# Later token placement in the expert phase and a one-bank, deeper pipeline in the second layer

## The chip, the cores and the metric

One Trainium2 chip, one of its cores. The metric is the device time of one execution in microseconds (us), the median over runs of the same kernel.

## What is computed

Sixteen sequences of 256 tokens with 256 features each (4096 tokens) pass two layers. The first is cross attention with 16 heads to a context of 120 rows per sequence, then a mixture of eight experts of which every token takes two. The second is cross attention with one head and a mask, then a linear layer whose input and weight are rounded in blocks of 32. All four parts are added to their own input, and each begins with a layer norm. Cut to its core:

```python
def reference(x, ctx_1024, mask_BxSxS2_ik1, ...):
    x = x + _L0_xattn_ref(_layernorm(x), ctx_1024, L0_xattn_Wq, L0_xattn_Wkv)
    x = x + _L0_ffn_ref(_layernorm(x), L0_ffn_W1, ..., L0_ffn_beta)
    x = x + _L1_xattn_ref(_layernorm(x), ctx_1024, ctx_1024, mask_BxSxS2_ik1, ...)
    x = x + _L1_ffn_ref(_layernorm(x), L1_ffn_weight, L1_ffn_bias)

def _L0_ffn_ref(...):
    probs = softmax(flat @ gate_W); topk_w, topk_idx = top_k(probs, 2)
    out = 0.5 * gelu(flat @ shared_W + shared_b)
    for e in range(8):
        out = out + combine[:, e:e+1] * (gelu(flat @ W1[e] + b1[e]) @ W2[e] + b2[e])
    # then a layer norm with gamma and beta

def _L1_xattn_ref(q, k, v, mask, Wq, Wk, Wv):
    Z = where(mask == 0, -1e9, (q@Wq) @ (k@Wk).T / 16);  return softmax(Z) @ (v@Wv)

def _L1_ffn_ref(x, weight, bias):
    xd, wd = rounded in blocks of 32 to a 6-bit grid, scaled back
    return xd @ wd.T + bias
```

## The kernel before

The program has three phases, one after the other on every engine: `attention_phase` (first layer's attention, up to about 305 us), `expert_phase` (to about 830 us) and `second_phase` (the rest). The order of the work on each engine is written out by hand. Engines meet only through semaphores: a wait blocks everything behind it on that engine.

**Expert phase.** The 8192 token copies are sorted by expert and cut into `SLOT_TILES` = 71 tiles of 128 rows. One tile n takes, on TensorE (PE), `first_product(n + 1)` (two halves of 16 matmuls), `turn_rows(n + 2)` (transposes of gathered rows) and `second_product(n)` (16 matmuls). VectorE (DVE) copies the tile's first weights (`tile_weights`, L1669) and adds bias and weight to the result (`finish`, L1682 and L1686). ScalarE (ACT) runs gelu (L1751).

Which rows a tile holds is found in two steps. `put` (L415, its DMA at L423) places 128 copies at a time: each of 128 descriptors writes 8 bytes (row number and weight) into the table `buckets` in DRAM. The first half of the tokens is placed during the attention phase, the second half (groups `THIRD` and `LAST`, 32 puts) in the expert loop on GpSimd (POOL). `slots` (L1426, on the SyncE queue SP) then fetches a tile's 128 entries into `b_slots`, in parts given by `PARTS`; with them POOL gathers the tile's rows (`gather`, L1509) and adds its results to `ffn_rows` in DRAM (`scatter`, L1520). Tiles 0 to 23 (`EARLY_TILES`) hold tokens of the first half alone; tile 24 and later need all puts to have landed.

POOL's loop over n: gather(n + 3), up to two puts, a scatter (from n = 9 on, two at every fourth n from 16), more puts. Puts start at n = `PUT_AT` = 5, with 5/2 a tile. The first puts wait for the places and weights that DVE makes at n = 4. In the same stretch SP carries 16 chunks of the shared branch through SBUF (load L1453, gelu on ACT L1460, store L1465), two chunks a tile up to n = 7; the first scatter waits until all are stored.

**Second phase.** It works on 16 batches of 256 tokens, each engine in `CYCLES` of one batch at several stages. For a batch n:

- DVE: `stats_acc`, `centre`, `residual` (L2058: x3, the input of the layer), `stats_x3`; `bounded` (L2089 scores with mask, L2093 maximum), `attended` (L2122: x4 = x3 + attention / sum of probabilities), `stats_x4`, `scales` (block maxima L2102 to L2109)
- POOL: `inverse_std` three times (norms of acc, x3, x4), `to_blocks` (L2004), `scale_back` (L2013)
- ACT: `normalise_x3` and `normalise_x4` (both L2154), `exps` (L2199), copies out of PSUM: `keep_xnT` (L2175), `keep_probsT` (L2209), `keep_xdT` (L2225), `keep_result` (L2232); `round_blocks` (L2217) and `lay_bias` (L2241, which writes the bias into the result's PSUM bank)
- PE: `turn_rows` (L2315), `scores` (L2345), `turn_probs` (L2355, transposes), `weigh` (L2365, attention times values), `start_result` (L2285, adds x4 to the result's bank by an identity matmul), `turn_quantised` (L2275), `linear` (L2295)

Of each context come keys (L2324) and values (L2332), after a transpose (L2303). The first `EARLY` = 7 contexts are worked before the cycles, while the last scatters land; contexts 7 to 15 inside them, one a cycle.

Of the kernel before, what the change touches and what calls it, by code (L numbers as in the profile page):

```python
# [1327 lines left out]
def expert_phase(nc, sem, past, routing, starts, ident, w1_sb, w2_sb, b1_rows, s_b12, b2, s_w1, s_w2,  # L1328
# [9 lines left out]
    with st:  # L1338
# [3 lines left out]
        def ps(name, shape, dt=F32):  # L1342
# [9 lines left out]
                 (EARLY_TILES, 40), (40, NS))  # L1352
# [50 lines left out]
        PUT_AT = 5  # L1403
# [109 lines left out]
        def gpsimd(pool):  # L1513
# [17 lines left out]
            for n in range(1, NS):  # L1531
                if n + AHEAD - 1 < NS:
# [3 lines left out]
                        range(5 * at // 2, min(5 * (at + 1) // 2, 4 * routing.GT))  # L1536
# [256 lines left out]
def second_phase(nc, sem, past, ident, second, mask, x2_d, acc_d, ctx, out):  # L1793
# [7 lines left out]
    with st:  # L1801
# [26 lines left out]
        x4, xn4 = ring("c_x4_", T2, n=2), ring("c_xn4_", T2, n=2)  # L1828
# [5 lines left out]
        tie = sb("c_tie", [P, 1])  # L1834

# [29 lines left out]
        g_bank = ps("c_g_ps", [P, 512])  # L1865
        g_ps = g_bank[:, 0:KC * CTX].rearrange("p (k c) -> p k c", k=KC)
# [3 lines left out]
        o_ps = ps("c_o_ps", T2)  # L1870
        xdT_ps = ps("c_xdT_ps", [P, 2, KC, P])
        f_ps = ps("c_f_ps", T2)
# [24 lines left out]
        s_o_p = sem("c_attn_psum")  # L1897
        s_rs = sem("c_rs_ready")
        s_x4 = sem("c_x4_ready")
        s_xn4 = sem("c_xn4_ready")  # L1900
        s_fb = sem("c_result_bias_set")
# [24 lines left out]
        CYCLES = range(-3, B + 3)  # L1926
# [3 lines left out]
        EARLY = 7  # L1930
# [4 lines left out]
        def sync(sp):  # L1935
# [25 lines left out]
            for n in range(RING):  # L1961
                load_x2(n)
            for s, value in past["added"]:
                sp.wait_ge(s, value)
            for n in range(RING):
                load_acc(n)
            for n in range(CTX_RING, B):
                load_context(n)
            for c in CYCLES:
# [3 lines left out]
                if exists(c + 5) and c + 5 >= RING:  # L1973
                    load_acc(c + 5)
                    load_x2(c + 5)
            for i in range(2):
                sp.wait_ge(s_ost[i], 8 * B)

        def gpsimd(pool):
# [38 lines left out]
            pool.memset(tie[:], TIE * FP8_DOWN).then_inc(s_tie, 1)  # L2018
            for c in CYCLES:
                scale_back(c - 2)  # L2020
                inverse_std(N4, c - 1, s_xn4)
                inverse_std(N3, c + 1, s_xn3)
                to_blocks(c - 1)
                inverse_std(NA, c + 3, s_x3)

        def vector(dve):
# [23 lines left out]
            def residual(n):  # L2050
# [5 lines left out]
                dve.wait_ge(s_x2_in[n % RING], loaded(n))  # L2056
                for u in range(2):
# [18 lines left out]
            def stats_x4(n):  # L2076
                if not exists(n):
                    return
                dve.wait_ge(s_x4, n + 1)
                stats(N4, x4[n % 2], n)  # L2080
# [30 lines left out]
            def attended(n):  # L2111
                if not exists(n):
                    return
                i = n % 2
                dve.wait_ge(s_e, n + 1)
                dve.reciprocal(rs[i][:], psum_[i][:]).then_inc(s_rs, 1)
                dve.wait_ge(s_rs, n + 1)
                dve.wait_ge(s_o_p, n + 1)
                ge(dve, s_f_p, n - 1)
                ge(dve, s_xn4, n - 1)  # L2120
                for u in range(2):
                    j = dve.scalar_tensor_tensor(out=x4[i][:, u, :], in0=o_ps[:, u, :],  # L2122
                                                 scalar=rs[i][:, u:u + 1], in1=x3[n % RING][:, u, :],
                                                 op0=ALU.mult, op1=ALU.add)
                j.then_inc(s_x4, 1)
# [13 lines left out]
            for c in CYCLES:  # L2139
                bounded(c)  # L2140
                stats_acc(c + 3)
                residual(c + 2)
                scales(c - 1)
                stats_x3(c + 2)
                attended(c)
                stats_x4(c)
                centre(c + 3)

        def scalar(act):
# [14 lines left out]
            def normalise_x4(n):  # L2164
# [3 lines left out]
                normalise(N4, xn4, x4, n, s_xn4)  # L2168
# [14 lines left out]
            def keep_keys(n):  # L2183
                act.wait_ge(s_g_p, n + 1)
                act.copy(gT[n][:], g_ps).then_inc(s_g, 1)
# [17 lines left out]

            def keep_probsT(n):
# [6 lines left out]
            def round_blocks(n):  # L2211
                if not exists(n):
                    return
                act.wait_ge(s_tie, 1)
# [12 lines left out]
            def keep_result(n):  # L2227
# [4 lines left out]
                act.copy(o[n % 2][:], f_ps[:]).then_inc(s_o, 1)  # L2232

            def lay_bias(n):
                if not exists(n):
                    return
                if n == 0:
                    act.wait_ge(second["s_vec"], 32)
                    act.wait_ge(s_fb, 1)
                ge(act, s_o, n)  # L2240
                act.copy(f_ps[:], fb[:].unsqueeze(1).broadcast_to(T2)).then_inc(s_fb, 1)  # L2241
# [7 lines left out]
            for c in CYCLES:  # L2249
                n = c + EARLY  # L2250
                exps(c)
                normalise_x4(c - 1)
                if late(n + 2):
                    keep_keys(n + 2)
                keep_probsT(c)
                normalise_x3(c + 1)
                keep_result(c - 2)
                lay_bias(c - 1)
                if late(n + 3) and n + 3 > EARLY:
                    keep_context(n + 3)  # L2260
                round_blocks(c - 1)
                keep_xnT(c + 1)
                if late(n + 1):
                    keep_values(n + 1)
                keep_xdT(c - 1)

        def tensor(pe):
            def turn_quantised(n):
                if not exists(n):
                    return  # L2270
                pe.wait_ge(s_xd, n + 1)
# [7 lines left out]
            def start_result(n):  # L2279
                if not exists(n):  # L2280
                    return

                pe.wait_ge(s_x4, n + 1)
                pe.wait_ge(s_fb, n + 2)
                pe.matmul(f_ps[:].rearrange("p u d -> p (u d)"), ident[:],  # L2285
                          x4[n % 2][:].rearrange("p u d -> p (u d)"),
# [133 lines left out]
```

## Time and profile before

| | us |
|---|---|
| median of 3 runs | 990.2 (989.22 to 990.7) |
| the profiled execution | 992.3 |
| its span, first to last instruction | 990.5 |
| PE busy | 934.2 (94%) |
| DVE busy | 530.0 (54%) |
| ACT busy | 517.7 (52%) |
| POOL busy | 495.2 (50%) |

The page's 40 slices show busy tenths per slice of 24.8 us:

```profile
PE   6999999999989979999999999999999999898885
DVE  3787898788874533452322323222232323899972
ACT  4777777677754723333343333333333333588774
PEclk9999999999999989999999999999999999999999
```

PE is full through the expert phase (slices 13 to 33), but for slice 15 (347 to 371 us), where it shows a 7 and the granted clock an 8. In the last six slices, the second phase, DVE is as full as PE or fuller.

### The profile page before, as it was taken

The numbers are of one execution on the slowest core, as the hardware profiler recorded it, in microseconds if no ns is written. First come the engines' busy times: TensorE is split into PE (matmuls) and PEld (weight loads), VectorE is DVE, ScalarE is ACT, GpSimd is POOL, SyncE is SP. The second block draws the span as 40 slices with busy tenths as digits, with TensorE's granted clock in tenths as the row PEclk, the third lists the DMA queues.
The fourth block names the chain that finished last, engine by engine and source line by source line (L and its number), as shares of the span: only waits on it lengthen the run. The fifth ranks groups of instructions, "written<-read, shape, count | busy, mean of one in ns | idle before, by whom it ended". The sixth has DMA issues, their size and how long they took to land. (4 is left out here: it accounts for less than half of the span.)

```text
span 990.5 us, 22054 instructions
## 1 busy us (share of the span) xinstructions
PE 934.2 (94%) x7133; PEld 797.3 (80%) x7133; DVE 530.0 (54%) x1300; ACT 517.7 (52%) x1310; POOL 495.2 (50%) x659
## 2 busy tenths in 40 slices
PE   6999999999989979999999999999999999898885
PEld 4777777676768969989999999999999998676653
DVE  3787898788874533452322323222232323899972
ACT  4777777677754723333343333333333333588774
POOL 3444344565653155775554443434444442577773
PEclk9999999999999989999999999999999999999999
DMA  5244453354533354433432221222222227433301
GB/s 179 77 124 149 134 177 122 114 152 141 151 118 108 115 136 68 53 32 47 55 59 44 38 44 27 32 40 32 44 33 39 38 41 188 129 97 97 96 33 43
DMA packets 86127, 85.39 MB, mean 86 GB/s; under 512 B 19296, under 2 KB 81184, under 8 KB 85888
## 3 DMA queue, kind: packets, MB, share of 16 engines
q1 hardware_dynamic: 70336, 65.28, 22.1%
q0 software_dynamic: 15680, 18.69, 12.8%
q8 instruction: 62, 1.02, 0.5%
q14 instruction: 49, 0.40, 0.2%
HBM read 52.54 MB, written 31.39 MB: 85 GB/s over the span
## 5 line engine op out<-in xcount | busy, mean ns | idle before, releaser
L1751 ACT ACTIVATE b_hiddenT<-b_H,b_b 128x128 f32<-128x128 f32 x568 | 161.8, 368 | 330.2 <-PE b_H L1581 293.8
L1581 PEld LDWEIGHTS b_H<-b_rowsT,b_w 128*128 128x128 f32 x2272 | 265.5, 192 | 12.2 <-issue 5.3
L1581 PE MATMUL b_H<-b_rowsT,b_w 128*128 128x128 f32 x2272 | 267.5, 275 | 6.4 <-issue 4.1
L1602 PE MATMUL b_Y<-w_sb,b_hiddenT 128*128 x1136 | 258.4, 381 | 1.1 <-ACT b_hiddenT L1751 0.6
L1520 POOL DMA_INDIRECT ffn_rows<-b_y,b_slots x71 | 140.5, 1979 | 197.2 <-DVE b_y L1686 121.1
L1602 PEld LDWEIGHTS b_Y<-w_sb,b_hiddenT 128*128 128x128 f32 x1136 | 211.5, 191 | 27.6 <-issue 1.4
L1682 DVE TENSOR_TENSOR b_y<-b_Y,b_b 128x256 f32<-128x256 f32 x71 | 30.2, 425 | 309.6 <-PE b_Y L1602 260.7
L1669 DVE COPY b_w<-w_sb 128x2048 f32 x71 | 87.3, 1230 | 35.5 <-issue 31.7
L1509 POOL DMA_INDIRECT b_rows<-xn_rows,b_slots x71 | 75.7, 1067 | 53.7 <-PE b_xT L1570 33.7
L1243 ACT COPY a_probsT<-a_T 120x512 f32<-120x512 f32 x128 | 74.7, 585 | 47.7 <-PE a_T L939 38.5
L423 POOL DMA_INDIRECT buckets<-r_pay,r_place x64 | 68.3, 1067 | 47.0 <-DVE r_pay L373 20.4
L939 PE MATMUL a_T<-ident,a_probs 128*120 128x128 f32 x512 | 77.9, 280 | 3.3 <-ACT a_probs L1235 3.1
L1076 DVE TENSOR_REDUCE a_max<-a_S 128x8 f32<-128x960 f32 x64 | 73.6, 1150 | 13.1 <-PE a_S L919 12.7
L1084 DVE TENSOR_TENSOR a_probs<-a_S,a_max 128x960 f32<-128x960 f32 x64 | 73.2, 1144 | 0.7
L939 PEld LDWEIGHTS a_T<-ident,a_probs 128*120 128x120 f32 x512 | 57.5, 139 | 16.0 <-issue 9.3
L1235 ACT ACTIVATE a_probs<-a_probs 128x960 f32<-128x960 f32 x64 | 64.5, 1007 | 8.3 <-DVE a_probs L1084 6.4
L953 PE MATMUL a_O<-a_probsT,a_vaug 120*32 120x128 f32 x1024 | 54.7, 287 | 0.5 <-ACT a_probsT L1243 0.3
L953 PEld LDWEIGHTS a_O<-a_probsT,a_vaug 120*32 120x32 f32 x1024 | 20.4, 108 | 29.3 <-issue 23.5
L785 POOL TENSOR_TENSOR a_x<-a_x,a_xin 128x256 f32<-128x256 f32 x16 | 12.4, 772 | 49.0 <-DVE a_x L1097 44.0
L988 PE MATMUL a_M<-a_wsg,a_xn2T 128*128 128x264 f32 x128 | 35.6, 401 | 0.2 <-ACT a_xn2T L1258 0.2
L919 PE MATMUL a_S<-a_kbd,a_qT 32*128 32x240 f32 x512 | 35.0, 387 | 0.9 <-ACT a_qT L1219 0.8
L2154 ACT ACTIVATE c_xn<-c_x,c_x_nb,c_x_rstd 128x256 f32<-128x256 f32 x64 | 34.8, 593 | 0.4 <-POOL c_x_nb L1995 0.3
(232 smaller groups left out, 1293.6 us busy)
## 6 DMA issues: line engine op xcount, KB each, us to landing
w_sb<-in_L_ffn_W SPq DMA_DIRECT2D x32, 512.0 KB
x_rows<-a_x SPq DMA_DIRECT2D x32, 128.0 KB
xn_rows<-a_xn SPq DMA_DIRECT2D x32, 128.0 KB
shared_rows<-a_shared SPq DMA_DIRECT2D x32, 128.0 KB
b_spare<-shared_rows SPq DMA_DIRECT2D x16, 256.0 KB
ffn_rows<-b_spare SPq DMA_DIRECT2D x16, 256.0 KB
c_x<-x_rows SPq DMA_DIRECT2D x16, 256.0 KB
c_acc<-ffn_rows SPq DMA_DIRECT2D x16, 256.0 KB, 2.9
```

Source lines behind the costliest of these rows:

```text
L423: pool.indirect_dma_start(bucket_d, IndirectOffsetOnAxis(place[:, t, k:k + 1], 0), pay[:, t, k, :], None).then_inc(s_put[g // 2], 16)
L939: i = pe.transpose(T_ps[q % 2][0:CTX, j * P:(j + 1) * P], pr[q // 2][:, 4 * (q % 2) + j, :], ident[:])
L953: i = pe.matmul(O_ps[VB * j:VB * (j + 1), q * P:(q + 1) * P], vaug[t // 2 % 2][0:CTX, 4 * q + j, :], pT[q % 2][0:CTX, j, :], start=True, s ...
L1076: dve.tensor_reduce(mx[h][:].rearrange("p (r j) -> p r j", r=RG), scores_of(h), AX.X, ALU.max).then_inc(s_mx, 1)
L1084: dve.tensor_tensor(pr[h][:].rearrange("p (r j) c -> p r j c", r=RG), scores_of(h), mx[h][:].rearrange("p (r j) -> p r j", r=RG).unsqueeze ...
L1243: act.copy(pT[q % 2][0:CTX].rearrange("p j n -> p (j n)"), T_ps[q % 2][0:CTX, :]).then_inc(s_T, 1)
L1509: pool.indirect_dma_start(xg[n % AHEAD][:], None, xn2_d, IndirectOffsetOnAxis(iw[:].bitcast(I32)[:, n, 0:1], 0)).then_inc(s_x[n % AHEAD], 16)
L1520: pool.indirect_dma_start(acc_d, IndirectOffsetOnAxis(iw[:].bitcast(I32)[:, n, 0:1], 0), y[n % KEPT_Y][:], None, bounds_check=TOK + SPARE - 1,
L1581: j = pe.matmul(H_ps[i][:, c * P:(c + 1) * P], w1c[i][:, k * HID + c * P:k * HID + (c + 1) * P], xT[:, k * P:(k + 1) * P], start=(k == 0), ...
L1602: j = pe.matmul(y_ps[i][:, 0:D], hT[i][:, c * P:(c + 1) * P], w2_sb[:, bass.ds(e * (HB * D) + c * D, D)], start=(c == 0), stop=(c == HB - 1))
L1669: dve.tensor_copy(w1c[i][:], w1_sb[:, bass.ds(e * (KC * HID), KC * HID)])
L1751: j = act.activation(hT[i][:, c * P:(c + 1) * P], H_ps[i][:, c * P:(c + 1) * P], ACT.Gelu, bias=b1c[i][:, c:c + 1])
```

## The change

1. **Placement.** `PUT_AT` goes from 5 to 8 and the rate from 5/2 to 8/3 puts a tile, so the puts are issued at n = 8 to 19 (before: 5 to 17). `PARTS` cuts the last 47 tiles into (24, 28), (28, 44), (44, 71) where it had (24, 40), (40, 71).
2. **One PSUM bank a batch.** There are three result banks `f_ps`. `start_result` (now first) lays x3 into the batch's bank, `weigh` adds attention to it there (making x4 in PSUM), and `linear` adds a bias matmul (one row of ones times the bias, 512 columns) and the four products. DVE's `attended` and its SBUF tile x4 are gone, and ACT's `lay_bias` too. `stats_x4` and `normalise_x4` read the bank.
3. **Division by the sums.** `inverse_sums` (DVE) takes the reciprocal, `diagonals` (ACT, two activations 128x128) makes a diagonal matrix of it, and `turn_probs` becomes a matmul with that matrix in place of the identity.
4. **Order.** The pipeline is one or more cycles deeper (`range(-4, B + 4)`), and every engine's order is new. `EARLY` is 9; a late context's keys and values are copied by ACT a cycle after PE made them; late keys share a bank with the contexts' transposes. SP loads contexts 8 and 9 ahead of the wait for the last scatter, and accumulator rows three cycles earlier.

```diff
-        PARTS = (..., (19, EARLY_TILES), (EARLY_TILES, 40), (40, NS))
+        PARTS = (..., (19, EARLY_TILES), (EARLY_TILES, 28), (28, 44), (44, NS))
-        PUT_AT = 5
+        PUT_AT = 8
-                        range(5 * at // 2, min(5 * (at + 1) // 2, 4 * routing.GT))
+                        range(8 * at // 3, min(8 * (at + 1) // 3, 4 * routing.GT))
...
-        EARLY = 7
+        EARLY = 9
...
             for c in CYCLES:      # POOL
-                scale_back(c - 2)
-                inverse_std(N4, c - 1, s_xn4)
-                inverse_std(N3, c + 1, s_xn3)
-                to_blocks(c - 1)
-                inverse_std(NA, c + 3, s_x3)
+                inverse_std(NA, c + 3, s_x3)
+                inverse_std(N3, c + 2, s_xn3)
+                to_blocks(c - 1)
+                inverse_std(N4, c, s_xn4)
+                scale_back(c - 1)
...
             for c in CYCLES:      # DVE
                 bounded(c)
-                stats_acc(c + 3)
                 residual(c + 2)
+                inverse_sums(c)
+                stats_x3(c + 2)
+                centre(c + 3)
                 scales(c - 1)
-                stats_x3(c + 2)
-                attended(c)
+                stats_acc(c + 4)
                 stats_x4(c)
-                centre(c + 3)
...
+            def diagonals(n):     # ACT
+                act.wait_ge(s_rs, n + 1)
+                for u in range(2):
+                    j = act.activation(dg[n % 2][:, u, :], ident[:], ACT.Identity,
+                                       scale=rs[n % 2][:, u:u + 1])
+                j.then_inc(s_dg, 1)
...
             for c in CYCLES:      # ACT, all lines new
+                exps(c - 1)
+                normalise_x4(c - 2)
+                diagonals(c - 1)
+                if late(c + 9):
+                    keep_keys(c + 9)
+                keep_result(c - 4)
+                keep_probsT(c - 1)
+                if late(c + 9):
+                    keep_values(c + 9)
+                keep_xdT(c - 3)
+                keep_xnT(c)
+                if EARLY < c + 10 < B:
+                    keep_context(c + 10)
                 normalise_x3(c + 1)
+                round_blocks(c - 2)
...
             def start_result(n):  # PE
-                pe.wait_ge(s_x4, n + 1)
-                pe.wait_ge(s_fb, n + 2)
+                pe.wait_ge(s_x3, n + 1)
+                ge(pe, s_o, n - 2)
                 # identity times x3 (before: x4), start=True
             def linear(n):
                 pe.wait_ge(s_xdT, n + 1)
+                pe.matmul(f_ps[n % RING][:], ones[0:1, :],
+                          fb[0:1, :].unsqueeze(1).broadcast_to([1, 2, D]),
+                          start=False, stop=False, skip_group_check=True)
...
             for c in CYCLES:      # PE, all lines new
+                turn_quantised(c - 3)
+                turn_probs(c - 1)
+                start_result(c - 1)
+                weigh(c - 1)
+                if EARLY < c + 10 < B:
+                    turn_context(c + 10)
+                scores(c)
+                linear(c - 3)
                 turn_rows(c + 1)
+                if late(c + 10):
+                    keys(c + 10)
+                if late(c + 10):
+                    values(c + 10)
```

## Rows read from the trace of the kernel before

**Rows 1.** Windows: stretch, its length, then busy us (instructions) of PE, PEld, DVE, ACT, POOL, granted PE clock, DMA share, GB/s. Expert phase.

```profile
600.00:700.00 100.00, 100.00 (x695) 94.40 (x694) 29.20 (x56) 34.56 (x123) 43.09 (x26) 1.00 0.22 35
...
331.55:339.15 7.60, 7.60 (x61) 7.17 (x60) 4.19 (x14) 4.84 (x12) 0.00 (x0) 1.00 0.25 71
...
346.40:355.29 8.89, 7.92 (x62) 7.06 (x61) 4.07 (x13) 2.60 (x10) 6.98 (x7) 1.00 0.63 141
355.29:371.82 16.53, 10.74 (x50) 8.96 (x51) 3.82 (x14) 4.47 (x13) 7.43 (x8) 0.79 0.54 137
371.82:379.07 7.25, 7.25 (x52) 6.83 (x50) 2.08 (x4) 2.54 (x9) 4.62 (x4) 1.00 0.43 96
```

**Rows 2.** Timeline, 338 to 376 us: start, length, engine, line, instruction, idle before.

```profile
343.11 1.05 POOL L423 DMA_INDIRECT buckets<-r_pay,r_place  x1 [20.40 <-DVE r_pay L373]
...
353.83 1.14 ACT L1751 ACTIVATE b_hiddenT<-b_H,b_b 128x128 f32<-128x128 f32 x4 [4.23 <-remote]
...
364.67 0.42 DVE L1682 TENSOR_TENSOR b_y<-b_Y,b_b 128x256 f32<-128x256 f32 x1 [12.66 <-remote]
...
373.54 2.61 POOL L1520 DMA_INDIRECT ffn_rows<-b_y,b_slots  x1 [8.68 <-issue]
```

**Rows 3.** DMA queues from 354 to 355 us: packets, MB, share of 16 engines.

```profile
q0 software_dynamic: 16, 0.07, 124.3%
```

**Rows 4.** Timelines of SP and POOL: the last 47 fetches of slots, the gather of tile 24.

```profile
446.58 53.16 SPq L1426 DMA_DIRECT2D b_slots<-buckets  x47
...
466.13 1.57 POOL L1509 DMA_INDIRECT b_rows<-xn_rows,b_slots  x1 [1.38 <-DMA b_slots<-buckets]
```

**Rows 5.** Windows of the second phase: four periods with contexts, eight without.

```profile
867.00:899.10 32.10, 30.59 (x185) 25.03 (x184) 29.90 (x101) 26.20 (x69) 23.14 (x49) 1.00 0.32 100
...
906.44:968.21 61.77, 49.80 (x262) 36.71 (x261) 52.92 (x184) 47.89 (x113) 44.12 (x94) 1.00 0.22 72
```

**Rows 6.** Groups by line, 845 to 990 us: busy us, mean ns of one, idle before.

```profile
L2122 DVE SCALAR_TENSOR_TENSOR c_x<-c_o_ps,c_rs,c_x 128x256 f32<-128x256 f32 x32 | 14.0, 480 | 2.6 <-PE c_o_ps L2365 2.0
...
L2058 DVE SCALAR_TENSOR_TENSOR c_x<-c_centred,c_acc_rstd,c_x 128x256 f32<-128x256 f32 x30 | 12.8, 467 | 0.0
L2199 ACT ACTIVATE c_probs<-c_z,c_nmax 128x120 f32<-128x120 f32 x32 | 12.4, 388 | 4.1 <-DVE c_nmax L2093 4.1
```

**Rows 7.** Timeline, a period without contexts: linear, weigh, and what PE starts next.

```profile
931.69 1.89 PE L2295 MATMUL c_f_ps<-c_wdT,c_xdT 128*128 128x256 f32 x8
...
933.42 1.03 PE L2365 MATMUL c_o_ps<-c_v,c_probsT 120*128 120x256 f32 x4
...
934.28 0.60 PE L2315 MATMUL c_xnT_ps<-ident,c_xn 128*128 128x128 f32 x4
```

**Rows 8.** Timeline, the second phase's beginning: rows, scores, z of batch 0, keys, values.

```profile
849.81 0.66 PE L2315 MATMUL c_xnT_ps<-ident,c_xn 128*128 128x128 f32 x4 [0.57 <-ACT c_xn L2154]
...
851.24 1.12 PE L2345 MATMUL c_zp_ps<-c_gT,c_xnT 128*128 128x120 f32 x8 [0.56 <-ACT c_xnT L2175]
...
852.20 1.06 PE L2324 MATMUL c_g_ps<-c_ctxT,c_wkq 128*128 128x120 f32 x8
852.40 0.41 DVE L2089 SCALAR_TENSOR_TENSOR c_z<-c_zp_ps,c_bound 128x240 f32<-128x240 f32 x1 [2.27 <-PE c_zp_ps L2345]
...
853.09 1.03 PE L2332 MATMUL c_v_ps<-c_wv,c_ctxT 128*120 128x256 f32 x4
```

**Rows 9.** Timeline, batch 15 to the end: z, stats and norm of x4, linear, result.

```profile
968.21 0.41 DVE L2089 SCALAR_TENSOR_TENSOR c_z<-c_zp_ps,c_bound 128x240 f32<-128x240 f32 x1 [0.81 <-PE c_zp_ps L2345]
...
974.07 0.75 DVE L2032 BATCH_NORM_STATS2 c_x_bn<-c_x 128x6 f32<-128x256 f32 x2
...
976.96 1.09 ACT L2154 ACTIVATE c_xn<-c_x,c_x_nb,c_x_rstd 128x256 f32<-128x256 f32 x2 [0.30 <-POOL c_x_nb L1995]
...
983.77 3.49 PE L2295 MATMUL c_f_ps<-c_wdT,c_xdT 128*128 128x256 f32 x8 [0.68 <-ACT c_xdT L2225]
987.30 0.59 ACT L2232 COPY c_out<-c_f_ps 128x512 f32<-128x512 f32 x1 [3.58 <-PE c_f_ps L2295]
```

More of the change, by code:

```diff
@@ L1869, in second_phase @@
         pT_ps = zp_ps[0:CTX, 256:512].rearrange("p (u n) -> p u n", u=2)
-        o_ps = ps("c_o_ps", T2)
-        xdT_ps = ps("c_xdT_ps", [P, 2, KC, P])
-        f_ps = ps("c_f_ps", T2)
+        f_ps = [ps(f"c_f_ps{i}", T2) for i in range(RING)]
         s_acc_in = [sem(f"c_acc{i}_loaded") for i in range(RING)]
@@ L1924, in loaded @@
             return 16 * (n // RING) + 16
-        CYCLES = range(-3, B + 3)
-        EARLY = 7
+        CYCLES = range(-4, B + 4)
+        EARLY = 9
         def late(n):
@@ L1962, in sync @@
                 load_x2(n)
+            for n in range(CTX_RING, CTX_RING + 2):
+                load_context(n)
             for s, value in past["added"]:
@@ L1966, in sync @@
                 load_acc(n)
-            for n in range(CTX_RING, B):
+            for n in range(CTX_RING + 2, B):
                 load_context(n)
-            for c in CYCLES:
+            for c in range(-5, B + 4):
                 if exists(c - 2):
@@ L2109, in scales, with inverse_sums @@
                 dve.reciprocal(rsc[i][:], sc[i][:]).then_inc(s_rsc, 1)
-            def attended(n):
+            def inverse_sums(n):
                 if not exists(n):
                     return
-                i = n % 2
                 dve.wait_ge(s_e, n + 1)
[L2116 to L2125, printed above, removed]
+                ge(dve, s_dg, n - 1)
+                dve.reciprocal(rs[n % 2][:], psum_[n % 2][:]).then_inc(s_rs, 1)
             def bounds(part):
@@ L2184, in keep_keys @@
                 act.wait_ge(s_g_p, n + 1)
-                act.copy(gT[n][:], g_ps).then_inc(s_g, 1)
+                act.copy(gT[n][:], late_g_ps if late(n) else early_g_ps).then_inc(s_g, 1)
             def keep_values(n):
@@ L2231, in keep_result @@
                 ge(act, s_ost[n % 2], 16 * (n // 2))
[L2232 to L2241, printed above, removed]
+                act.copy(o[n % 2][:], f_ps[n % RING][:]).then_inc(s_o, 1)
             load_exp_and_log(nc, act)
@@ L2320, in keys @@
                 pe.wait_ge(s_ctxT, n + 1)
-                ge(pe, s_g, n)
+                if not late(n):
+                    ge(pe, s_g, n)
+                at = late_g_ps if late(n) else early_g_ps
                 for m in range(KC):
                     for k in range(KC):
-                        j = pe.matmul(g_ps[:, m, :], wkq[:, k, m * P:(m + 1) * P],
+                        j = pe.matmul(at[:, m, :], wkq[:, k, m * P:(m + 1) * P],
                                       ctxT[n % 2][:, k, :], start=(k == 0), stop=(k == KC - 1))
@@ L2375, in tensor @@
                 pe.wait_ge(s, value)
-            pe.matmul(f_ps[:].rearrange("p u d -> p (u d)"), ident[:],
-                      wdT[:].rearrange("p k d -> p (k d)"), start=True, stop=True,
-                      skip_group_check=True).then_inc(s_fb, 1)
             for c in CYCLES:
-                n = c + EARLY
-                turn_probs(c)
-                linear(c - 2)
-                weigh(c)
-                turn_rows(c + 1)
-                if late(n + 4) and n + 4 > EARLY:
-                    turn_context(n + 4)
-                start_result(c - 1)
-                scores(c + 1)
-                turn_quantised(c - 1)
-                if late(n + 3):
-                    keys(n + 3)
-                if late(n + 2):
-                    values(n + 2)
+                turn_quantised(c - 3)
[6 more added lines that the diff above has]
+                linear(c - 3)
+                turn_rows(c + 1)
+                if late(c + 10):
+                    keys(c + 10)
+                if late(c + 10):
+                    values(c + 10)
         return Programs(sync, gpsimd, tensor, vector, scalar)
```

74 lines of the change are left out of this document (37 added, 37 removed).

## The prediction

> **What bounds the kernel now.** I read the 40 slices first, then the windows. In the expert phase PE is busy 100.00 of 100 us at full clock, a tile in 7.25 us [rows 1]: there only PE time counts, and everything else is hidden until it makes PE wait. At one place it does. The two tiles from 346.40 to 371.82 took 8.89 and 16.53 us. A tile without a count takes 7.25 and one with a count 7.60; the first of the two holds a count. So 25.42 - 14.85 = 10.6 us are lost, part of it at a granted clock of 0.79 [rows 1]. Beside it ACT waited 4.23 us and DVE 12.66 us for something the profile can't name ("remote") [rows 2]. In one of these microseconds 16 packets of GpSimd's queue held all 16 DMA engines (124%) while moving 0.07 MB [rows 3]. So the DMA side was congested, not short of bandwidth.
>
> In the second phase DVE sets the pace without contexts: 8 periods in 61.77 us, 7.72 each, DVE busy 52.92 of them, and most of what is left is the small gap after each of its instructions [rows 5]. With contexts 32.10 us hold four periods, 8.0 each, and PE is busy 30.59 of them, 7.65 a period [rows 5]: PE bounds those. I count from z of batch 0 at 852.40 to z of batch 15 at 968.21, 115.8 us for 15 periods [rows 8, 9], and 22.3 us from there to the end of the span, 990.5.
>
> **Part 1, placement.** Before, POOL stood 20.40 us for DVE, put from 343.11 on, and had issued 12 puts and four gathers when it reached its first scatter, which began at 373.54 [rows 2]. These 12 puts lie exactly on the stall, while 16 chunks of 256 KB are carried by SP in the same stretch. Chunks ran from 310 us on without puts, and the tile from 331.55 took its 7.60; later puts ran without chunks, and the tile from 371.82 took 7.25 [rows 1]. Both together are the suspect. After the change POOL reaches n = 8 about when the places are ready anyway (it runs up to three tiles ahead of PE), so puts still begin near 344 us; but only four of them stand ahead of the first scatter (two at n = 8, two at n = 9), which waits for the last chunk. The gather of tile 9 no longer stands behind puts. Two ends: -10.6 us (all of the stall) and 0 (it isn't the puts). I take **-10.6**, since four puts in some 20 us are nearer to the stretch with none than to twelve.
>
> What it could cost: 8/3 puts of about 1.3 us with their gap, a gather of about 1.3 and a scatter of about 1.9 make 6.7 us a tile, under 7.25. The last put moves two tiles back, 14.5 us, less the 10.6: +3.9. So the fetches of `b_slots` behind it, which began at 446.58, begin near 450.5; they take 53.16 / 47 = 1.13 us each [rows 4], and only 4 instead of 16 now stand before the gather of tile 24. That gather came at 466.13 after a wait of 1.38 [rows 4]; now it can come near 457. PE turns these rows at n = 22, fourteen tiles after n = 8 at 361, so near 465 to 469. Cost 0; if POOL or SP were some 8 us later than that, each further us would be lost.
>
> **Part 2, the second phase's start.** The accumulator rows arrive as before, and normalised rows of batch 0 are transposed at 849.81 [rows 8] as before: two more early contexts (1.96 us each on PE, which stood idle there) end just before. But PE now has keys(9) and values(9) behind these transposes (1.06 + 1.03 us [rows 8]), and ACT must copy both out before it copies the transposed rows: 850.4 + 1.8 + 0.4 + 0.6 = 853.2 for the first scores, which were at 851.24. **+2.0.**
>
> **Part 3, periods.** DVE loses `attended` (two of 480 ns [rows 6], about 0.9 with the gap): its 7.72 [rows 5] become 6.8. ACT loses a bias copy (a copy of that shape took 0.59 [rows 9]) and gets two diagonals; not shown before, bounded by the gelu row, 1.14 for four, so 0.51 for two [rows 2], and two exps at 388 ns [rows 6], 0.78; I take 0.63. PE gets the bias matmul: one row deep, but 512 columns as in weigh's (four passes of 256 over two operands, 0.86 from start to next start [rows 7]). I take **0.86**; the low end, 0.6, would be the four transposes [rows 7].
>
> With contexts PE is the bound: 7.65 + 0.86 = 8.5 a period. That is worse than 8.0, but contexts are in fewer cycles; three of them fall where all of PE's steps exist (batches 3 to 6): 25.5.
>
> Without contexts PE needs 49.80 / 8 = 6.2 [rows 5] + 0.86 = 7.1 and DVE 6.8. But the new order closes a loop through all engines: `normalise_x4(c)` stands on ACT ahead of `diagonals(c + 1)`. Step by step: weigh ends, 0.1 to DVE; from its statistics to ACT's norm 2.89 (974.07 to 976.96), the norm 1.09 [rows 9]; the diagonals 0.63; `keep_result` 0.59 [rows 9], for which `start_result` waits (three banks); `start_result` 0.86; weigh 1.03 [rows 7]; two hand-overs 0.06. Sum **7.25**. `turn_probs` and the copy of probabilities run beside `start_result`. Low end 7.0 (diagonals 0.51, steps that overlap 0.1 each), high 7.6. Nine periods: 65.3.
>
> The first three lack steps: batch 0 to 1 has no norm of x4 in the loop (6.2), the next two no result to copy but keys (7.0 each): 20.2. Sum 20.2 + 25.5 + 65.3 = 111.0 against 115.8: **-4.8**.
>
> `stats_x4` now reads PSUM. No row shows these statistics from PSUM; the nearest pair is L2122 (PSUM) at 480 and L2058 (SBUF) at 467 ns [rows 6], so 0.03 for two, and I count nothing. The Trainium skill, "VectorE: DVE Perf Modes", section on the TRN2 errata, gives a PSUM source 120 cycles where SBUF has 58, at 0.96 GHz; by that estimate two instructions cost 0.13 more a period and the sum would be about 2 us higher. The pair of rows speaks against it.
>
> **Part 4, the end.** From z of batch 15 the chain is the old one up to `stats_x4`, but with the norm of batch 14 and a result copy ahead of `weigh`: +0.4. Then `linear` stands behind its own bias matmul: +0.86, or +1.7 at half clock. The old last linear took 3.49 us [rows 9] where others took 1.89 [rows 7], so it ran at the lower clock. PE has more to do in the last 10 us now (a whole linear runs later), so the clock may stay up, worth -1.6. Ends -0.3 and +2.1, I take **+0.9**.
>
> Sum against the profiled execution: -10.6 + 2.0 - 4.8 + 0.9 = -12.5, a span of 978.0. The profiled execution took 992.3, 2.1 over the median; I subtract the same from the median: 990.2 - 12.5 = **977.7**.
>
> **Rivals.**
> *B, the stall stays.* The puts are bystanders and PE starves on something that the chunks, or the place in the program, bring. For it: the four puts that remain begin at the same time, ACT was late at 350, after only four or five puts [rows 2], and the gaps are named by no semaphore. Against it: the clean tiles on either side. Then only the second phase moves: 990.2 - 1.9 = 988.3. The Trainium skill, "Runtime: NRT & Kernel Launch", section on instruction fetch, says that crossing a block of 16 KiB of instructions is mostly hidden. If it holds, late code is no cause here either; if it does not, transfers of any kind could hold code up and B gains. No row tells which.
> *C, half of it goes.* Four puts and the chunks still hold PE for some 5 us: 983.
> *D, slower.* The stall stays and the loop of part 3 is longer: POOL must serve the norm of x4 at once, and `to_blocks(c - 1)` stands ahead of it. If it, or ACT's queue, is late by 0.65 a period, the nine periods take 7.9 each, +5.9: 994.2. It decides from a loop of 7.67 on, with the stall in place; with the stall gone, not even 8.1 makes the kernel slower.
>
> **How the numbers follow.** As forecast 0.50, C 0.14, B 0.26, D 0.10. A measurement of this kernel tells about 0.2% (2 us) from no change. B lies at that border and is split: faster 0.50 + 0.14 + 0.13 = 0.77, same 0.13 + 0.01 = 0.14, slower 0.09. The forecast's own range is 974 (loop 7.0, end -0.3) to 982 (loop 7.6, end +2.1). The range of 8 in 10 takes in C and B: 974 to 990.
>
> **What would show it.** Windows of the tiles from 346 on: all near 7.25 or 7.60, PE without "issue" gaps; the first scatter near 364 instead of 373.54; the expert phase ending near 819; tile 24's gather well ahead of PE. In the second phase: the first scores 3.4 us after the first transposes of rows (before 1.43); results copied every 8.5 us, then every 7.25; DVE's wait before `stats_x4` on weigh, ACT's before `normalise_x4` on POOL. Wrong if a gap of the same size stands elsewhere in the expert phase, if gathers wait for `b_slots` near tile 24 or 28, or if results come 7.7 us or more apart.

## The result and the profile after

| | before | after |
|---|---|---|
| median, us | 990.45 (989.22 to 990.73) | 978.17 (973.1 to 984.82) |
| the profiled execution, us | 992.3 | 978.93 |
| its span, us | 990.5 | 977.2 |

The ratio of after to before is 0.9878, 95% interval 0.9846 to 0.9911: 12.1 us less (8.8 to 15.3 by the interval). The prediction said 977.7. The page's slices of after, 24.4 us each:

```profile
PE   6999999999989999998999999999999999899997
...
DVE  3788898888874543533223223232232232787862
...
PEclk9999999999999999999999999999999999999999
```

The slice with a 7 and a granted clock of 8 is gone from the expert phase, and in the second phase PE is fuller and DVE emptier. Windows of after: two tiles of the old stall's place, then three periods with contexts, eight without, and the end. The columns are those of [rows 1].

```profile
344.91:353.07 8.16, 7.75 (x61) 7.24 (x61) 4.03 (x13) 3.60 (x11) 4.38 (x5) 1.00 0.57 159
353.07:360.32 7.25, 7.25 (x51) 6.83 (x50) 3.81 (x14) 3.60 (x11) 0.44 (x1) 1.00 0.71 235
...
864.69:891.46 26.77, 26.73 (x149) 20.59 (x150) 19.22 (x70) 20.70 (x55) 17.60 (x36) 1.00 0.30 90
898.43:954.31 55.88, 55.88 (x289) 41.95 (x289) 44.73 (x165) 46.39 (x119) 41.69 (x88) 1.00 0.26 80
954.31:977.20 22.89, 17.43 (x62) 10.45 (x61) 4.34 (x17) 9.09 (x20) 7.76 (x13) 0.93 0.13 46
```

The first two answer to 8.89 and 16.53 us in [rows 1]: 8.16 and 7.25, the clock at 1.00. The next two answer to [rows 5]: 8.92 a period where it was 8.0, and 6.98 where it was 7.72.

GpSimd and SyncE around the puts. Two puts stand at 343.62 and 345.80, two more at 351.25 and 352.54; then comes the first scatter, 11 us earlier than in [rows 2]. The gather of tile 24 is at 457.29 and waits for no slots (466.13 in [rows 4]).

```profile
343.62 1.88 POOL L423 DMA_INDIRECT buckets<-r_pay,r_place  x1 [0.30 <-issue]
...
352.54 0.97 POOL L423 DMA_INDIRECT buckets<-r_pay,r_place  x1 [0.30 <-issue]
362.49 2.15 POOL L1521 DMA_INDIRECT ffn_rows<-b_y,b_slots  x1 [8.98 <-issue]
...
450.21 19.91 SPq L1427 DMA_DIRECT2D b_slots<-buckets  x18
...
457.29 1.03 POOL L1510 DMA_INDIRECT b_rows<-xn_rows,b_slots  x1 [0.30 <-issue]
```

The second phase's beginning, which answers to [rows 8]: transposes of batch 0, keys and values of context 9, ScalarE's copy, the first scores.

```profile
839.89 0.63 PE L2325 MATMUL c_xnT_ps<-ident,c_xn 128*128 128x128 f32 x4 [1.54 <-ACT c_xn L2154]
840.35 1.05 PE L2336 MATMUL c_ctxT_ps<-c_ctxT,c_wkq 128*128 128x120 f32 x8
...
841.24 1.03 PE L2344 MATMUL c_v_ps<-c_wv,c_ctxT 128*120 128x256 f32 x4
...
842.57 0.59 ACT L2175 COPY c_xnT<-c_xnT_ps 128x512 f32<-128x512 f32 x1
...
843.31 1.12 PE L2357 MATMUL c_zp_ps<-c_gT,c_xnT 128*128 128x120 f32 x8 [0.83 <-ACT c_xnT L2175]
```

The scores begin 3.42 us after the transposes; before it was 1.43. One round of the loop in the steady part (weigh to weigh) reads:

```profile
924.34 1.03 PE L2377 MATMUL c_f_ps<-c_v,c_probsT 120*128 120x256 f32 x4
...
925.41 0.76 DVE L2040 BATCH_NORM_STATS2 c_x_bn<-c_f_ps 128x6 f32<-128x256 f32 x2 [0.34 <-PE c_f_ps L2377]
...
928.17 1.02 ACT L2154 ACTIVATE c_xn<-c_f_ps,c_x_nb,c_x_rstd 128x256 f32<-128x256 f32 x2
928.20 0.75 DVE L2040 BATCH_NORM_STATS2 c_x_bn<-c_x 128x6 f32<-128x256 f32 x2
...
929.09 0.69 ACT L2211 ACTIVATE c_diagonal<-ident,c_rs 128x128 f32<-128x128 f32 x2
...
929.67 0.58 ACT L2243 COPY c_out<-c_f_ps 128x512 f32<-128x512 f32 x1
...
930.39 1.10 PE L2287 MATMUL c_f_ps<-c_x,ident 128*128 128x512 f32 x2
...
931.33 1.03 PE L2377 MATMUL c_f_ps<-c_v,c_probsT 120*128 120x256 f32 x4
```

The row at 928.20 stands beside the loop (statistics of x3, from SBUF). Each of the others starts as the one before it hands over, and the sum is 6.99.

**The spans by stage.** The stages are cut at four points: the start of PE's first second product in the expert phase (near 304, the column "first"), the end of its last one, z of batch 0, z of batch 15. "Expert" is from the first of these to the second, "start" from there to z of batch 0, "periods" to z of batch 15, "tail" to the span's end. The kernels below the first two are the experiments'. They ran in three groups on three chips; in each the kernel before was timed beside them.

| kernel | group (time of before) | first | expert | start | periods | tail | span |
|---|---|---|---|---|---|---|---|
| before | | 305.38 | 524.08 | 22.94 | 115.81 | 22.3 | 990.5 |
| after | | 303.88 | 515.67 | 24.92 | 109.84 | 22.9 | 977.2 |
| placement_alone | A (990.7) | 303.42 | 513.38 | 22.94 | 115.79 | 20.8 | 976.4 |
| second_alone | A | 305.20 | 523.71 | 24.92 | 109.82 | 22.7 | 986.3 |
| after_again | A (990.3) | 302.40 | 512.70 | 24.92 | 109.75 | 23.2 | 973.0 |
| put7 | B (975.1) | 299.89 | 512.57 | 24.92 | 109.80 | 23.4 | 970.5 |
| put6 | B | 300.98 | 512.41 | 25.01 | 109.79 | 23.2 | 971.4 |
| before_again | C (1001.3) | 311.59 | 524.37 | 23.39 | 115.84 | 23.1 | 998.3 |
| put6_again | C | 312.83 | 523.87 | 24.92 | 109.77 | 23.4 | 994.8 |

Between the first two rows: -1.5 in code that the change doesn't touch, -8.4 expert, +2.0 start, -6.0 periods, +0.6 tail, -13.3 in all.

### The profile page after: what moved, and what is told of

Read it like the earlier page. It is cut to its first block, busy times and chain, and to the rows that moved or that the text cites. A ratio compares the mean times of both kernels' runs of the same rounds, so it can differ in the third digit from the quotient of the medians.

```text
span 977.2 us, 22166 instructions
## 1 busy us (share of the span) xinstructions
PE 944.5 (97%) x7195; PEld 804.6 (82%) x7195; DVE 515.9 (53%) x1268; ACT 519.7 (53%) x1326; POOL 495.2 (51%) x660
## 4 chain that ended last, share of the span: by engine, by line
PE 88%; DVE 3%; issue 2%; ACT 2%; POOL 2%; another core or an unknown queue 1%; SPq 1%; DMA 1%; DVEq 0%; POOLq 0%; ACTq 0%
PE b_H L1582 25%; PE b_Y L1603 24%; PE a_T L939 5%; PE a_O L953 4%; PE c_f_ps L2303 3%; PE a_S L919 3%; PE a_M L988 3%; PE a_O L894 2%; PE c_f_ps L2298 2%; PE b_xT L1571 2%; PE a_T L905 2%; PE c_f_ps L2287 1%; PE c_zp_ps L2357 1%; PE c_f_ps L2377 1%
## 5 line engine op out<-in xcount | busy, mean ns | idle before, releaser
L423 POOL DMA_INDIRECT buckets<-r_pay,r_place x64 | 70.6, 1103 | 24.4 <-issue 19.4
L953 PEld LDWEIGHTS a_O<-a_probsT,a_vaug 120*32 120x32 f32 x1024 | 20.2, 108 | 28.9 <-issue 23.1
L2303 PEld LDWEIGHTS c_f_ps<-c_wdT,c_xdT 128*128 128x128 f32 x128 | 23.4, 193 | 14.8 <-issue 12.1
```

The source lines that it names most:

```text
L423: pool.indirect_dma_start(bucket_d, IndirectOffsetOnAxis(place[:, t, k:k + 1], 0), pay[:, t, k, :], None).then_inc(s_put[g // 2], 16)
L953: i = pe.matmul(O_ps[VB * j:VB * (j + 1), q * P:(q + 1) * P], vaug[t // 2 % 2][0:CTX, 4 * q + j, :], pT[q % 2][0:CTX, j, :], start=True, s ...
```

## The experiments

**Each part alone.** The first is the kernel before with the placement, the second the kernel after without it.

```diff
-        PARTS = (..., (EARLY_TILES, 40), (40, NS))
+        PARTS = (..., (EARLY_TILES, 28), (28, 44), (44, NS))
-        PUT_AT = 5
+        PUT_AT = 8
-                        range(5 * at // 2, min(5 * (at + 1) // 2, ...
+                        range(8 * at // 3, min(8 * (at + 1) // 3, ...
```

> The kernel before with the placement part alone (puts from n = 8, 8/3 a tile, the new parts); the second phase is the old one. Theory, the puts ahead of the first scatter make the stall: the expert phase's tiles after the first with puts take 7.25 or 7.60, a span about 10.6 us shorter than before less the small waits that the trace after shows later (2.55 us at 446.71), so 8 to 10 us shorter: 980.5 to 982.5. Rival, the stall belongs to the chunks or to that place in the program: 990 as before, and the 8.4 us that the expert phase gained in the trace after come from elsewhere.

> The kernel after with the placement of before (puts from n = 5, 5/2 a tile, the old parts), so the second-phase part alone. Theory: the stall near 350 to 371 us is back, and the second phase gives what the trace after shows, start +1.8, periods -6.0, tail +0.6, so -3.6: 986.8. My prediction had -1.9, so 988.3. Rival, the stall was chance or moved with the phase: near 978.

The placement alone took 979.2 us, ratio 0.9887 (0.9833 to 0.9942); one of its four executions took 1893 us, for no reason that a record shows, and the ratio leaves it out. The second phase alone took 989.2, ratio 0.9992 (0.9968 to 1.0015). Windows of two tiles of each, from second product to second product, the old place of the stall:

```profile
349.05:356.39 7.34, 7.34 (x51) 6.93 (x51) 3.23 (x15) 2.83 (x9) 3.23 (x3) 1.00 0.71 203
356.39:363.63 7.24, 7.24 (x52) 6.83 (x51) 3.30 (x6) 3.59 (x11) 1.61 (x1) 1.00 0.44 141
```

```profile
350.80:368.72 17.92, 12.23 (x51) 10.88 (x51) 2.71 (x11) 3.70 (x12) 10.50 (x11) 0.66 0.51 110
368.72:376.72 8.00, 8.00 (x51) 7.39 (x51) 3.90 (x10) 3.50 (x11) 2.24 (x2) 0.90 0.32 101
```

The first fence is the placement alone, the second the second phase alone. On this chip the stall comes and goes with the placement and with nothing else of the change: with four puts ahead of the first scatter instead of twelve it is gone. Which part of the placement does it (the later start, the rate, or `PARTS`) was not separated here. The second phase's gain is smaller in the times (1.5 us between the medians, and the interval takes in no change) than in the stages of the two traces (3.6, from +2.0, -6.0 and +0.4). This difference is not explained. The executions with the stall spread widely, 987.1 to 994.9 for before beside these two, against 973.1 to 976.7 for before in group B, below. There put7, without a stall, gains 3.9. The waits of the second kernel there, 340 to 385 us, have the same names as in [rows 2]:

```profile
DVE b_y L1683 <- remote: 14.9, 1, 14.9
ACT b_hiddenT L1752 <- remote: 14.6, 2, 9.1
PE b_H L1582 <- issue: 5.7, 7, 1.9
```

**How many puts.** The kernel after with puts from n = 7 and from n = 6, both at 5/2 a tile. That is seven and, counted in the trace, nine puts ahead of the first scatter; the expectation says ten for the latter.

```diff
-        PUT_AT = 8
+        PUT_AT = 7        # put6: 6
-                        range(8 * at // 3, min(8 * (at + 1) // 3, ...
+                        range(5 * at // 2, min(5 * (at + 1) // 2, ...
```

> The kernel after with puts from n = 7 at 5/2 a tile: seven puts ahead of the first scatter, where after has four and before twelve. If the lost time grows with the puts that are issued in one row there (10.0 us at twelve, about none at four), three tiles lose 4 us: 982. If there is a threshold below twelve, all 10 (988) or nothing (978).

> The kernel after with puts from n = 6 at 5/2 a tile: ten puts ahead of the first scatter. Lost time in proportion: 7.5 us, 985.5. Threshold: 10 (988) or nothing (978).

Measured 971.2 and 973.0, but the kernel before beside them took 975.1 (ratios 0.9961, 0.9950 to 0.9972, and 0.9975, 0.9956 to 0.9995). Neither trace has a stall: the expert phase takes 512.6 and 512.4. So the kernel before and put6 were run once more, which was on a third chip.

> The kernel before, unchanged, for a second look at its trace. Beside the last four kernels the kernel before took 975.1 us where it had taken 990.7 beside the first four. Theory, the stall of the expert phase is what differs: if it takes about 975 here, the second products around 350 us follow each other by 8.1, 7.3 and 7.3 us and there is no stall; if it takes about 990, they follow by 8, 16 and 8.5. Rival, the whole program runs faster or slower by some other cause: 16 and 8.5 either way.

> The kernel after with puts from n = 6 at 5/2 a tile once more. If the kernel before takes about 990 beside it (it has the stall): in proportion to the puts ahead of the first scatter it loses some 7.5 us and takes 985; if fewer than twelve are enough to make it vanish, 978; if the stall comes at ten as at twelve, 988. If the kernel before takes about 975 beside it, no stall and 971 to 973 as before.

Measured 1000.0 for the kernel before (1001.3 in the runs beside it). Put6 ran twice, 996.5 and 986.0, ratio 0.9889 (0.9751 to 1.0026), which is not clear of no change. The trace is that of the execution with 996.5. The same code of put6 on the chip of group B and on that of group C, the tile after the same second product:

```profile
346.63:353.97 7.34, 7.34 (x50) 6.93 (x51) 3.81 (x14) 2.90 (x9) 5.82 (x6) 1.00 0.74 108
```

```profile
358.44:372.53 14.09, 10.65 (x51) 9.42 (x51) 3.77 (x15) 3.69 (x12) 6.58 (x7) 0.81 0.62 132
```

And the waits beside the second of them, 340 to 385 us:

```profile
DVE b_y L1683 <- remote: 9.5, 1, 9.5
ACT b_hiddenT L1752 <- remote: 4.1, 1, 4.1
```

Two things follow. The stall is a matter of the chip, too: nine puts cost nothing on one chip and, on another, 6.8 us at this place, 0.7 in the next tile and 3.7 two tiles after that; the expert phase is 11.5 longer in all (523.87 against 512.41). The waits for something "remote" say the same: every trace of groups A and C has one of over 1 us in the expert phase, and none of the four traces of group B has. And in this execution the loss isn't in proportion to the puts: nine puts cost as much as twelve did in before_again, in more places. That is one execution. The other took 10.5 us less and has no trace, so the size of the loss may change from execution to execution, and how it depends on the number of puts isn't settled. After, with its four puts, wasn't run on this chip. Whether before has no stall on the chip of group B wasn't profiled. Its time leaves no room for one of this size: put7 takes 971.2 there, and the stages of the second phase make before 3 to 4 us longer than that, which is 975.

**After beside before once more.**

> The kernel after, unchanged, beside the kernel before, for the ratio of the two where the kernel before takes another time. Theory, the second-phase part gives 3.6 us everywhere and the placement gives what the stall costs there: if the kernel before takes about 975 here, after takes 971.4 (ratio 0.996); if 990.7, 978.5 (0.988); if 1001, 985 to 989 (0.984 to 0.988), with small stalls left. Rival, the gain is a fixed 12 us: 963 where before takes 975.

It ran on the chip of group A again: 977.7 against 990.3, ratio 0.9882 (0.9829 to 0.9935), as at first. Its expert phase took 512.70, 3.0 less than in the first trace of after. That one had one more wait, at 446.71, while puts, gathers and scatters follow each other and no chunk is carried any more:

```profile
443.02 1.14 ACT L1752 ACTIVATE b_hiddenT<-b_H,b_b 128x128 f32<-128x128 f32 x4 [6.90 <-remote]
...
446.71 0.49 PE L1582 MATMUL b_H<-b_rowsT,b_w 128*128 128x128 f32 x2 [2.55 <-ACT b_rowsT L1759]
```

It looks like the old stall in small: ScalarE waits for something "remote" while its input is there (PE's product ran from 436.26 to 439.99). Puts are still issued there, so this form comes without chunks. That the puts bring it here too is not shown.

**The bias.** One kernel leaves the bias matmul out, so its result lacks the last layer's bias. The other adds the bias as two bf16 parts (value and rest, on 32 rows each against 1/32) in one bf16 matmul, ahead of the wait for the rounded rows.

```diff
             def linear(n):
-                pe.wait_ge(s_xdT, n + 1)
-                pe.matmul(f_ps[n % RING][:], ones[0:1, :],
-                          fb[0:1, :].unsqueeze(1).broadcast_to([1, 2, D]), ...)
+                pe.wait_ge(s_xn4, n + 1)
+                pe.matmul(f_ps[n % RING][:], ones[0:64, :],      # bf16, 1/32
+                          fb2[0:64, :].unsqueeze(1).broadcast_to([64, 2, D]), ...)
+                pe.wait_ge(s_xdT, n + 1)
```

> The kernel after without the bias matmul; the result lacks the last layer's bias. In the trace after TensorE is busy all of the 55.88 us of the eight periods without contexts (6.98 each) and all of the periods with contexts (8.92), and the bias matmul takes 1.05 of each from start to next start. If TensorE bounds the periods: 7.87 with contexts; without contexts the next bound comes after 0.3 us or so (VectorE waits 0.34 for weigh in each period), so 6.65; tail 1.05 shorter: 978.2 - 3.2 - 3.0 - 1.1 = 971. If my loop through all engines sets the periods without contexts, they stay at 6.98 and the time is 974.

> The kernel after with the bias as two bf16 parts in one bf16 matmul (one pass over the 512 columns where fp32 takes four), ahead of the wait for the rounded rows instead of behind it; VectorE makes the parts once. If TensorE bounds the periods and the matmul takes a quarter, 0.25 us: 0.8 less a context period and 0.3 less another until the next bound, and 1.0 off the tail: 972. If the place or the type makes no difference: 978.

Measured 973.1, ratio 0.9847 (0.979 to 0.9903), and 971.8, ratio 0.9832 (0.9777 to 0.9887), in group A. By stage, the periods with contexts take 7.68 and 8.19 instead of 8.92, and the tail 21.2 in both instead of 22.9. The periods without contexts take 6.98 in both, exactly as with the fp32 bias. Eight of them without the bias, and two of PE's waits in them:

```profile
893.40:949.27 55.87, 50.01 (x274) 39.13 (x273) 44.78 (x164) 46.42 (x119) 41.60 (x88) 1.00 0.26 80
```

```profile
L2278 PE MATMUL c_xdT_ps<-ident,c_xd 128*128 128x128 f32 x32 | 5.2, 286 | 5.6 <-POOL c_xd L2020 5.6
L2364 PEld LDWEIGHTS c_zp_ps<-c_diagonal,c_probs 128*120 128x120 f32 x32 | 4.0, 182 | 2.2 <-ACT c_diagonal L2211 2.2
```

PE is free for 5.9 of 55.87 us and the period doesn't move. A busy PE (55.88 of 55.88 in after) wasn't what set it there. Nor is it the wait for POOL, though it is the longest: behind it PE's weight load waits another 0.27 a period for ScalarE's diagonals, and those are a step of the loop. With contexts a busy PE was the bound. The bf16 matmul's step in a context period, and that of the fp32 one in after's tail:

```profile
870.19 0.39 PE L2304 MATMUL c_f_ps<-c_bias_parts,c_ones 64*128 64x512 bf16 x1
870.51 1.99 PE L2310 MATMUL c_f_ps<-c_wdT,c_xdT 128*128 128x256 f32 x8
```

```profile
965.39 1.12 PE L2298 MATMUL c_f_ps<-c_fb,c_ones 1*128 1x512 f32 x2 [0.67 <-ACT c_xdT L2236]
966.44 2.90 PE L2303 MATMUL c_f_ps<-c_wdT,c_xdT 128*128 128x256 f32 x8
...
971.92 1.99 PE L2303 MATMUL c_f_ps<-c_wdT,c_xdT 128*128 128x256 f32 x8
```

From start to next start: 0.32 against 1.05. Either form also lengthens its neighbours: in a context period the scores ahead take 1.05 to the next start instead of 0.96, and `linear` behind 1.83 instead of 1.74. So the fp32 bias costs 1.05 + 0.19 = 1.24 and the bf16 one 0.32 + 0.19 = 0.51, which are the differences of the periods. The weight loads (PEld) show it. Without the bias, the load for `linear` began 0.10 ahead of its first matmul (L2300, 921.00 and 921.10). Behind the bias in after, PEld idles and starts with the matmul:

```profile
927.23 1.59 PEld L2303 LDWEIGHTS c_f_ps<-c_wdT,c_xdT 128*128 128x128 f32 x8 [0.76 <-issue]
927.24 1.99 PE L2303 MATMUL c_f_ps<-c_wdT,c_xdT 128*128 128x256 f32 x8
```

The kernel with the bf16 bias is faster than before. Against after the two intervals of group A overlap; below, in group B, it is clear.

**The loop.** One diagonal instead of two, used for both halves of the batch, so half of the probabilities are divided by another row's sum.

```diff
             def diagonals(n):
-                for u in range(2):
+                for u in range(1):
             def turn_probs(n):
-                    j = pe.matmul(pT_ps[:, u, :], pr[n % 2][:, u, :], dg[n % 2][:, u, :],
+                    j = pe.matmul(pT_ps[:, u, :], pr[n % 2][:, u, :], dg[n % 2][:, 0, :],
```

> The kernel after with one diagonal matrix made instead of two, used for both halves of a batch; so half of the probabilities are divided by another row's sum. ScalarE loses one 128x128 activation, 0.35 us, a period, and no other engine anything. Theory, the periods without contexts are set by the loop that goes through ScalarE (norm, diagonals, result copy) and so on to start_result and weigh: 6.98 becomes 6.65 (VectorE waits 0.34 a period for weigh in the trace after, and would bound them there), 9 periods, 3.0 us less than after. Rival, TensorE, busy all of the 6.98, or VectorE's own work sets them: 6.98 as before. The periods with contexts stay at 8.92.

Measured 974.7, ratio 0.984 (0.9792 to 0.9887), beside 977.7 for after. Two z of the steady part:

```profile
926.63 0.38 DVE L2098 SCALAR_TENSOR_TENSOR c_z<-c_zp_ps,c_bound 128x240 f32<-128x240 f32 x1
933.53 0.38 DVE L2098 SCALAR_TENSOR_TENSOR c_z<-c_zp_ps,c_bound 128x240 f32<-128x240 f32 x1
```

The period is 6.90, not 6.65. The first two periods, where PE has little to do, became 0.29 shorter each (5.99 and 6.64 for 6.28 and 6.93), so the loop through ScalarE was shortened by nearly its whole activation; in the steady part 0.08 of it is seen, since PE comes next. PE's steps in this trace, each from start to next start, add up to the period: bias 1.05, `linear` 1.83, three times four transposes at 0.44, `start_result` 0.86, weigh 0.865, scores 0.98, together 6.90. In after two of them are longer, `start_result` 0.93 and `turn_probs` 0.45, so 0.09 of the 6.98 are waiting although PE shows as busy all the time. So both theories hold, 0.08 us apart: the loop sets 6.98, PE's own work 6.90. My expectation had forgotten that second bound.

**The start.** One more early context, and this together with the bf16 bias.

```diff
-            for n in range(CTX_RING, CTX_RING + 2):
+            for n in range(CTX_RING, CTX_RING + 3):
-        EARLY = 9
+        EARLY = 10
```

> The kernel after with EARLY = 10 (and context 10 among those loaded ahead of the wait for the last scatter), so a tenth context before the cycles. Theory: keys(9) and values(9) no longer stand between the first transposes and the first scores, which come 1.4 us after them instead of 3.42, so the start is 1.8 to 2.0 shorter (24.9 to 23.0); and one period with a context at 8.92 becomes one without at 6.98, which is 1.9 less: 978.2 - 3.9 = 974.3. If TensorE ends the tenth context after the rows of batch 0 are there (it ended the ninth 1.8 us before), up to 0.2 of it is given back. Rival, the start is set by ScalarE's copies and not by TensorE's order: only 1.9 less, 976.3.

> Both edits, EARLY = 10 and the bias as one bf16 matmul ahead of the wait for the rounded rows. They touch different places but for one context period (8.19 with this bias): 971.8 - 1.9 - 1.2 = 968.7. If the two gains overlap: 970 to 972.

Measured 971.2, ratio 0.9975 (0.9953 to 0.9996), and 968.3, ratio 0.9930 (0.9913 to 0.9946), in group B, where put7 took 971.2: the tenth context gives nothing, and the bf16 bias gives 3.0. That 968.3 lies near the 968.7 expected is luck: the sum began from 971.8 of another chip and took off 3.1 for the tenth context. ScalarE and PE of early10 at batch 0:

```profile
833.76 0.37 ACT L2189 COPY c_v<-c_v_ps 120x256 f32<-120x256 f32 x1 [0.51 <-PE c_v_ps L2344]
834.03 1.09 ACT L2154 ACTIVATE c_xn<-c_x,c_x_nb,c_x_rstd 128x256 f32<-128x256 f32 x2
```

```profile
835.26 0.63 PE L2325 MATMUL c_xnT_ps<-ident,c_xn 128*128 128x128 f32 x4 [1.54 <-ACT c_xn L2154]
...
836.66 1.12 PE L2357 MATMUL c_zp_ps<-c_gT,c_xnT 128*128 128x120 f32 x8 [0.77 <-ACT c_xnT L2175]
```

The scores do come 1.40 after the transposes, as expected. But the transposes come 22.30 us after the last expert product instead of 20.34. ScalarE copies each early context out in turn, and batch 0's norm stands behind the last copy: nine contexts just fit, the tenth pushes the norm back by its own 1.96. And no context period went: the one that disappeared lies ahead of z of batch 0.

## Why the prediction was right, and where it wasn't

In the first pair of traces the four terms missed by +2.2 (placement), 0.0 (start), -1.2 (periods) and -0.3 (tail), and the attention phase, which the change leaves alone, moved by -1.5. So the mechanisms held in the main, and that the sum came out within 1 us is partly luck.

- **Placement, -10.6.** The main step held. The stall goes with the placement alone, and rival B (it stays) fell on the chip where both were seen: the second phase alone gives 989.2, near B's 988.3. Full size: 524.1 to 512.7, 11.4 us, of which some 10 at the place that I counted and the rest at two later tiles (0.5 and 0.9). In the first trace 3.0 of them were missing (the wait at 446.71 and its like). The signs came as written: first scatter at 362.49 (forecast near 364), four puts ahead of it, fetches of slots from 450.21 (450.5), tile 24's gather at 457.29 (457), end of the expert phase at 819.55 (819).
- **What the prediction didn't know.** It took the stall as a property of the kernel. It is one of kernel and chip, so it is luck that the sum met a chip that has the stall: group B has a kernel before of 975.1, and there put7, which is after but for the puts' start, gives 0.4%.
- **Start, +2.0.** Measured 1.98, by the steps given: transposes as before (20.34 after the last product against 20.35), scores two later.
- **Periods, -4.8.** Measured -6.0. First three 20.22 (20.2). Three with contexts 26.77 (25.5): the term that failed is the bias matmul, put at 0.86 by weigh's row. Its step is 1.05, and it adds 0.09 to the scores ahead of it and 0.10 to `linear` behind; without it the period is 7.68, almost my 7.65 of before, so it costs 1.24. Both ends of my bound, 0.6 and 0.86, were too low. Nine without contexts 62.85 (65.3): 6.98 a period, under my low end of 7.0. The loop was the right mechanism. Its steps overlap more than I allowed: norm of x4 to the diagonals 0.92 (1.09), the diagonals to the copy 0.58 (0.63), statistics to norm 2.76 (2.89 plus a hand-over); the copy to `start_result` is longer, 0.72 (0.59), and so is `start_result` to weigh, 0.94 (0.86). The two errors have opposite signs and left 1.2 us.
- **Statistics from PSUM.** 0.76 us for two from PSUM at 925.41 against 0.75 from SBUF at 928.20. That agrees with counting nothing. The Trainium skill, "VectorE: DVE Perf Modes", section on the TRN2 errata, would have had 0.13 more; this trace doesn't bear that out for this instruction.
- **Tail, +0.9.** Measured +0.6 in the first pair, but for another reason. I took 1.6 off for a clock that stays up. It fell one linear earlier: linear of batch 14 took 2.90, the last one 1.99. Where PE's clock stays at 1.00 through the last linear, the old tail is 20.8 (placement_alone) and the new one 21.8 (early10). So the chain costs 1.0, less than my 0.4 + 0.86, and the clock is luck on either side: the new tails with a fall and the fp32 bias are 22.7 to 23.4, and 26.6 in one_diagonal. With the bf16 bias and no fall the tail is 20.8 (early10_bias_bf16), as long as the old one.
- **C and D.** C (half of it goes) was not seen on the chip of group A; on that of group C, with nine puts, the first place lost 7.4 us where before lost 11.7, and another made up most of the rest. D needed a loop over 7.67; it is 6.98.

**What stays open.** What the engines wait for in the stall. In the second phase, the one bank, the order and the deeper pipeline were changed together and are not priced one by one. In before, one packet of an instruction queue was under way from 351.62 to 353.86 us, beside ScalarE's first wait; the next began at 375.81. Yet PE's 32 matmuls came in eight pieces from 355.29 to 365.1, with gaps named "issue", and so with no such packet under way. Code that arrives late doesn't show in these pieces; for ScalarE's first wait it isn't ruled out. What is shown: on the chip of group A the stall is there with the early puts and gone with the later ones, and GpSimd itself goes on issuing in it. Whether the chunks are needed for the large form wasn't tried: taking them away changes when the scatters start.

## What to carry to other kernels

Ask of a stall without a named releaser whether it comes on other chips as well, and put the kernel before beside each experiment: here the change is worth 1.2% on one chip and, as put7, 0.4% on another. Where small scattered writes share a stretch with other transfers, try fewer of them ahead of the next wait: here four instead of twelve took 11 us away on one chip. Spreading them is no guarantee, since one trace of after still lost 3 us among interleaved puts. Two bounds can lie 0.1 us apart, so a fully busy engine isn't yet the one that sets the period; take its work away and look. A matmul that only adds a row isn't cheap for being one row deep (1.24 us a context period here, 0.51 as two bf16 parts), so price it by its columns and type, and with what it adds to its neighbours.

## What was not expected of the hardware

- The same program took 975.1, 990.7 and 1001.3 us on three chips. Most of it lies ahead of the second phase: the first second product came at 299.9 to 302.0, 301.5 to 305.9 and 311.6 to 312.8 us, and the stall adds some 11.5 to the expert phase where it appears.
- An fp32 matmul one row deep with 512 columns took 1.05 us from start to next start, longer than weigh's 120 rows over the same columns, 0.87. With two bf16 parts it took 0.32. Either form added 0.19 to the steps beside it.
- In eleven of the fourteen traces the granted clock fell in the last 16 us, while PE still had a `linear` to do (not in placement_alone, early10 and early10_bias_bf16), to 0.50 (1.2 GHz; 1.0 is 2.4 GHz), at different points, in stretches where PE waited between short matmuls. In one_diagonal it stayed at 0.50 to the end, and its tail was 26.6 us.
